# Linear attention in a 16-part network: one masked copy of the queries for each tile, scores over 32 rows, values in two strips, and another draw of the order

## What is computed

```python
def titans_forward(hidden_states, Wq, Wk, Wv, conv_q, conv_k, conv_v, W_init, ln_gamma, ln_beta, Wg, Wo, num_heads=16, chunk_size=16):
    q = l2norm(jax.nn.silu(short_conv(hidden_states @ Wq.T, conv_q)).reshape(b, l, h, dk))
    ...
    def step(W, chunk):
        q_c, k_c, v_c = chunk
        inter = jnp.einsum('bqhk,bhkv->bqhv', q_c, W)
        qk = jnp.einsum('bqhd,bkhd->bhqk', q_c, k_c) * mask
        intra = jnp.einsum('bhqk,bkhv->bqhv', qk, v_c)
        W_new = W + jnp.einsum('bchk,bchv->bhkv', k_c, v_c)
        return (W_new, inter + intra)
    ...
    o = (o - mu) * jax.lax.rsqrt(var + EPS_LN) * ln_gamma + ln_beta
    gate = hidden_states @ Wg.T
    return o * gate @ Wo.T
```

## Time and profile before

| | before |
|---|---|
| median of 3 runs | 3529.78 us (3524.93 to 3536.67) |
| the profiled execution | 3542.59 us, span 3541.3 us, clock 0.933 |
| PE busy | 3005.1 us, 85% |
| DVE busy | 2370.4 us, 67% |
| ACT busy | 2252.9 us, 64% |
| POOL busy | 1280.5 us, 36% |
| granted TensorE clock, mean | 0.933 |
| instructions | 56793 |

### The profile page before, as it was taken

How to read it: one execution, slowest core, us unless ns; L and a number is a source line. 1 busy time by engine, 2 the same in 40 slices (tenths; PEclk the granted TensorE clock), 3 DMA queues, 4 the chain that set the end, 5 groups by cost and what they waited for, 6 DMA issues and landing times. The chain is left out here.

```text
span 3541.3 us, 56793 instructions
## 1 busy us (share of the span) xinstructions
PE 3005.1 (85%) x20199; PEld 1965.9 (56%) x20199; DVE 2370.4 (67%) x6076; ACT 2252.9 (64%) x4884; POOL 1280.5 (36%) x1196
## 2 busy tenths in 40 slices
PE   3577899898989999999998777787988879899997
PEld 2356666665645555555564454664746648555444
DVE  4888755566678777676777888776454443566655
ACT  3556564536756776667777775874847746567764
POOL 2555533523445643243564654443020120211221
PEclk9789999999999999999999998998999979899998
DMA  6444422222100012110101213554342234222320
GB/s 245 129 124 146 118 70 82 72 60 83 55 11 1 1 33 53 40 46 15 52 1 34 73 58 96 161 150 114 101 108 88 79 102 142 77 67 51 74 56 7
DMA packets 209444, 272.22 MB, mean 77 GB/s; under 512 B 39560, under 2 KB 147272, under 8 KB 207176
## 3 DMA queue, kind: packets, MB, share of 16 engines
q1 hardware_dynamic: 200968, 251.79, 24.5%
q0 software_dynamic: 8192, 16.79, 1.6%
HBM read 217.02 MB, written 54.00 MB: 77 GB/s over the span
## 5 line engine op out<-in xcount | busy, mean ns | idle before, releaser
L382 ACT ACTIVATE scratch<-psum 128x512 f32<-128x512 f32 (+7 forms) x1804 | 837.3, 495 | 695.4 <-PE psum L328 483.5
L328 PE MATMUL psum<-scratch 128*128 128x128 f32 (+14 forms) x8016 | 936.8, 321 | 110.8 <-ACT scratch L382 34.6
L474 POOL TENSOR_TENSOR scratch<-scratch 128x512 f32<-128x512 f32 (+3 forms) x536 | 615.1, 1162 | 753.1 <-PE psum L353 280.4
L328 PEld LDWEIGHTS psum<-scratch 128*32 128x32 f32 (+7 forms) x8016 | 592.4, 147 | 435.0 <-issue 192.4
L382 ACT ACTIVATE scratch<-scratch 128x512 f32<-128x512 f32 (+8 forms) x856 | 395.2, 468 | 230.9 <-DVE scratch L404 143.3
L374 ACT ACT_TABLE_LOAD x390 | 500.4, 1283 | 17.8 <-DVE scratch L404 8.0
L404 DVE TENSOR_TENSOR scratch<-psum,scratch 128x512 f32<-128x512 f32 (+3 forms) x712 | 381.2, 547 | 149.6 <-ACT scratch L382 109.3
L348 PE MATMUL psum<-w_constants,scratch 128*128 128x128 f32 (+1 forms) x1944 | 329.1, 290 | 48.9 <-ACT scratch L382 17.3
L418 DVE TENSOR_TENSOR_SCAN psum<-psum,scratch 128x512 f32<-128x512 f32 x256 | 309.2, 1222 | 70.4 <-ACT psum L382 59.9
L427 DVE TENSOR_REDUCE scratch<-psum 128x2 f32<-128x512 f32 (+2 forms) x336 | 225.0, 677 | 193.8 <-PE psum L328 158.2
L382 ACT ACTIVATE psum<-scratch 128x255 f32<-128x255 f32 (+1 forms) x528 | 221.2, 457 | 171.2 <-DVE scratch L404 161.1
(11 more groups left out here) (108 smaller groups left out, 4214.0 us busy)
## 6 DMA issues: line engine op xcount, KB each, us to landing
scratch<-b_and_c_out SPq DMA_DIRECT2D x256, 256.0 KB
scratch<-L_experts_rows_dram SPq DMA_DIRECT2D x56, 544.0 KB
scratch<-L_experts_rows_dram SPq DMA_DIRECT2D x56, 514.0 KB
slots_out<-scratch SPq DMA_DIRECT2D x112, 128.0 KB
q_stack<-scratch SPq DMA_DIRECT2D x72, 192.0 KB, 2.5
scratch<-q_out SPq DMA_DIRECT2D x96, 96.0 KB
scratch<-slots_in SPq DMA_DIRECT2D x16, 512.0 KB
q_out<-scratch SPq DMA_DIRECT2D x40, 192.0 KB, 3.0
```

The source lines that it names most:

```text
L328: return self.engine.matmul(out, lhsT, rhs, start=start, stop=stop, **kw)
L382: return self.engine.activation(out, src, function, **kw)
L474: return self.engine.tensor_tensor(out, a, b, op)
```

## The change

One constant now says which of four places within its group a channel has, for all groups at once, so a single masked copy `qm` holds for a tile what four copies did. The scores of group g take only the group's 32 rows of `k` and of this copy; 64 copies on POOL become 16. `st` gets three buffers, the third in `padded`, which is not used by then. The values of two groups form one step, `pe_intra`, in which the matmuls alternate between two 32-column strips of the array; PE's order in a tile is scores 0, 1, 2, values of groups 0 and 1, scores 3, values of groups 2 and 3. The seed of the draw is 3, and the planner takes the load of the masks to be complete 2000 ns later.

```diff
--- before.py
+++ after.py
@@ -70,7 +70,7 @@
 
 
     c["head_of_col_group"] = np.tile((ch[None] % 32 // HD8 == np.arange(4)[:, None]).astype(float).reshape(1, -1), (P, 1))
-    c["channels_of_head"] = (np.arange(HEADS8)[None] == ch[:, None] // HD8).astype(float)
+    c["place_in_group"] = (np.arange(4)[None] == ch[:, None] % 32 // HD8).astype(float)
     q, k = np.arange(P)[:, None], np.arange(P)[None]
     c["keys_up_to_query"] = (q <= k).astype(float)
 
@@ -514,7 +514,7 @@
 
 
 
-    LEFT, NEAR, DRAW = 0.4, 3.0, 20
+    LEFT, NEAR, DRAW = 0.4, 3.0, 3
 
     def __init__(self, nc, ctx):
         self.nc, self.ctx, self.draws = nc, ctx, np.random.RandomState(self.DRAW)
@@ -957,7 +957,10 @@
         self.v_tok, self.k_tok = self.take(TILES, P), self.take(PER_STREAM, P)
         self.state = self.take(P)
         self.o = self.v
-        self.qm, self.st, self.vm = [self.take(4, P), self.take(4, P)], self.take(4, P), self.take(4, P)
+        self.qm, self.vm = [self.take(4, P), self.take(4, P)], self.take(4, P)
+        mark = self.used
+        self.st = [self.take(4, P), self.take(4, P), v2(self.padded.rearrange("p a b -> p (a b)")[:, 0:4 * P], P)]
+        self.used = mark
         self.out_norm = Norm(self, "o", self["o", TILES - 1], self.o, self.o, self.c["center8"], self.c["mean8"],
                              eps[:, 0:1], self.w["ln_gamma"], self.w["ln_beta"])
 
@@ -990,23 +993,30 @@
                 e.wait_ge(*(yield self["o", t - 1]))
             e.matmul(self.b[:, 0:P], self.state if chunk else w["state0"], self.q[:, here], skip_group_check=True)
             for g in range(4):
-                rows = slice(32 * g, 32 * g + 32)
-                e.wait_ge(*(yield self["one_head", t, g]))
+                if g == 0:
+                    e.wait_ge(*(yield self["one_head", t]))
                 if g:
                     e.wait_ge(*(yield self["masked", t, g - 1]))
                 elif t:
                     e.wait_ge(*(yield self["masked", t - 1, 3]))
-                e.matmul(self.a, self.k[:, here], self.qm[g % 2].rearrange("p a b -> p (a b)")).then_inc(*self.post("scores", t, g))
-                e.wait_ge(*(yield self["masked", t, g]))
-                e.wait_ge(*(yield self["spread_v", t]))
-                for j in range(4):
-                    last = e.matmul(self.b[rows, 0:P], self.vm[:, j, rows], self.st[:, j, :], start=False, skip_group_check=True)
-                last.then_inc(*self.post("intra", t, g))
+                e.matmul(self.a, self.k[32 * g:32 * g + 32, here], self.qm[t % 2][32 * g:32 * g + 32].rearrange("p a b -> p (a b)")).then_inc(*self.post("scores", t, g))
+                if g >= 2:
+                    yield from self.pe_intra(e, t, g - 2)
         yield from self.out_norm.pe(e)
         e.wait_ge(*(yield self["normed", "o"]))
         e.matmul(self.a, w["Wg"], self.xn).then_inc(*self.post("gate"))
         e.wait_ge(*(yield self["gated"], None, (self.b, self["norm", "logvar", "o"])))
         e.matmul(self.b, w["Wo"], self.o).then_inc(*self.post("out"))
+
+    def pe_intra(self, e, t, pair):
+
+        e.wait_ge(*(yield self["masked", t, 2 * pair + 1]))
+        e.wait_ge(*(yield self["spread_v", t]))
+        for j in range(4):
+            for g in (2 * pair, 2 * pair + 1):
+                rows = slice(32 * g, 32 * g + 32)
+                last = e.matmul(self.b[rows, 0:P], self.vm[:, j, rows], self.st[(4 * t + g) % 3][:, j, :], start=False, skip_group_check=True)
+        last.then_inc(*self.post("intra", t, pair))
 
     def act(self, e):
         T = TOKENS
@@ -1023,7 +1033,7 @@
         e.wait_ge(*(yield self["tokens"]))
         e.activation(self.k_tok, v2(self.b[:, 0:PER_STREAM * P], P), ACT.Copy).then_inc(*self.post("token", "k_tok"))
         for t in range(TILES):
-            e.wait_ge(*(yield self["intra", t, 3]))
+            e.wait_ge(*(yield self["intra", t, 1]))
             e.activation(self.o[:, t * P:(t + 1) * P], self.b[:, 0:P], ACT.Copy).then_inc(*self.post("o", t))
         yield from self.out_norm.act(e)
 
@@ -1053,11 +1063,10 @@
                 e.tensor_tensor(self.state, self.state, w["state0"], ALU.add).then_inc(*self.post("state", t))
             for g in range(4):
                 e.wait_ge(*(yield self["scores", t, g]))
-                if g:
-                    e.wait_ge(*(yield self["intra", t, g - 1]))
-                elif t:
-                    e.wait_ge(*(yield self["intra", t - 1, 3]))
-                e.tensor_tensor(self.st, v2(self.a, P), over(self.c["keys_up_to_query"].unsqueeze(1), [P, 4, P]), ALU.mult).then_inc(*self.post("masked", t, g))
+                n = 4 * t + g - 3
+                if n >= 0:
+                    e.wait_ge(*(yield self["intra", n // 4, n % 4 // 2]))
+                e.tensor_tensor(self.st[(4 * t + g) % 3], v2(self.a, P), over(self.c["keys_up_to_query"].unsqueeze(1), [P, 4, P]), ALU.mult).then_inc(*self.post("masked", t, g))
         yield from self.out_norm.dve(e)
         e.wait_ge(*(yield self["gate"]))
         e.tensor_tensor(self.o, self.o, self.a, ALU.mult).then_inc(*self.post("gated"))
@@ -1066,18 +1075,16 @@
 
     def pool(self, e):
         e.wait_ge(*(yield self["normed", "k"]))
-        for n in range(4 * TILES):
-            t, g = divmod(n, 4)
-            if n >= 2:
-                e.wait_ge(*(yield self[("scores", *divmod(n - 2, 4))]))
-            q = self.q[:, t * P:(t + 1) * P]
-            e.tensor_tensor(self.qm[g % 2], over(q.unsqueeze(1), [P, 4, P]),
-                            over(self.c["channels_of_head"][:, 4 * g:4 * g + 4].unsqueeze(2), [P, 4, P]), ALU.mult).then_inc(*self.post("one_head", t, g))
-            if g == 0:
-                e.wait_ge(*(yield self["token", "v_tok"]))
-                if t:
-                    e.wait_ge(*(yield self["intra", t - 1, 3]))
-                e.tensor_tensor(self.vm, over(self.v_tok[:, t:t + 1, :], [P, 4, P]), v2(self.c["head_of_col_group"], P), ALU.mult).then_inc(*self.post("spread_v", t))
+        for t in range(TILES):
+            here = slice(t * P, (t + 1) * P)
+            if t >= 2:
+                e.wait_ge(*(yield self["scores", t - 2, 3]))
+            e.tensor_tensor(self.qm[t % 2], over(self.q[:, here].unsqueeze(1), [P, 4, P]),
+                            over(self.c["place_in_group"].unsqueeze(2), [P, 4, P]), ALU.mult).then_inc(*self.post("one_head", t))
+            e.wait_ge(*(yield self["token", "v_tok"]))
+            if t:
+                e.wait_ge(*(yield self["intra", t - 1, 1]))
+            e.tensor_tensor(self.vm, over(self.v_tok[:, t:t + 1, :], [P, 4, P]), v2(self.c["head_of_col_group"], P), ALU.mult).then_inc(*self.post("spread_v", t))
 
 
 def row_exp_dve(b, e, tag, ready, logits, out, m, n):
@@ -3197,7 +3204,7 @@
             e.dma_start(weights["constants"].buf, packed_dram["constants"]).then_inc(*core.post((0, "load", "constants"), 16, FIRST_LATENCY))
             first, *rest = [g for g in groups[1:] if g not in LATER]
             e.dma_start(weights[first].buf, packed_dram[first]).then_inc(*core.post((0, "load", first), 16, FIRST_LATENCY))
-            e.dma_start(staged, packed_dram["masks"]).then_inc(*core.post((0, "load", "masks"), 16, FIRST_LATENCY))
+            e.dma_start(staged, packed_dram["masks"]).then_inc(*core.post((0, "load", "masks"), 16, FIRST_LATENCY + 2000))
             e.dma_start(x[:, COLS:], x_dram[:, COLS:]).then_inc(*core.post((0, "load", "x_rest"), 16, FIRST_LATENCY))
             for g in rest:
                 e.dma_start(weights[g].buf, packed_dram[g]).then_inc(*core.post((0, "load", g), 16, LOAD_LATENCY))
```

## The result

The changed kernel takes 3547.1 us against 3532.4, the medians of 20 executions each: ratio 1.0041, interval 1.0029 to 1.0052. It is slower by 0.4%, 15 us, where a gain of 17 was forecast. Its profiled execution took 3550.4 us, span 3549.0, clock 0.925.

What follows compares the result with a forecast made beforehand. PE's time was taken as the first limit of the Linear stage, one stream's chain as the second. Of 20 us saved on PE 15 reach the end, with 2 from the start: -17, median 3529.8 to 3513; range 3482 to 3550.

Steps and rivals of the forecast that it cites:

- (6): Whole kernel: the new draw breaks ties differently, moving the end 18 us either way, centre 0.
- the sum: Whole kernel: 15 of 20 us saved on PE reach the end, plus 2 from the start: -17 us.
- (1): Linear's values on PE: 32 lots in two strips at 1.22 us replace 64 at 1.18; gain 36.5 us.
- The rival without overlap: Linear's values: strips do not run side by side, PE loses 13 us, time 3538; chance 0.03.
- (2): Linear's scores on PE: 32 rows lengthen each slot by 0.28 us, 64 times: 18 us of loss.
- the rival: Linear stage: emptier array lowers PE's clock; at 0.85 the kernel takes 3547 us; chance 0.09.
- point of balance: Linear stage: clock of 0.90, where PE's slowdown equals the 20 us saved.
- (3): One stream's Linear chain: a tile falls from 11.1 to 8.75 us, saving 10.6 us over four tiles.
- a sign of being wrong: After Linear: the prediction is wrong if Linear shortens and the lead is gone later.
- (4): POOL in Linear: 64 masked query copies become 16, 50 us less work, costed at nothing; bounds 0 to -2 us.
- (5): Kernel start on ACT: square precedes the masks' conversion, logarithm at 16.6 instead of 18.61, 2.0 us earlier.
- slower by the order: Outside the Linear stage: the draw costs its 18 us and more and eats the gain, 3550; chance 0.12.

Runs made afterwards that it cites:

- five orders: Five settings of seed or masks' due time, each run without and with the Linear edits in the full kernel; mean difference 0.05%, standard error 0.4%.
- Linear alone: Network replaced by eight Linear parts per stream, seed 3: 1536.3 us without edits, 1557.2 with all three, 1843.0 with only 32-row scores.
- strips alone: Linear-only kernel before plus values in pairs of strips and three masked copies of scores, scores on 128 rows, 64 query copies: 1308.6 us.

## Why the prediction was wrong

Two steps failed. Term (6) put the new draw at a centre of 0, and without any edit of Linear the new seed and due time made the kernel before 1.3% slower, about 45 us. And the sum let 15 us of PE's gain reach the end, where over five orders nothing did (2 us slower in the mean, standard error 14): the lower clock that comes with 32-row scores takes part of the gain, and the lead that remains is lost in later parts. Term by term:

- (1) Values in strips: right. Two strips run side by side, 36.6 us busy for 512 records; the slot is 1.19 by the forecast's own count (1.22 forecast), so the term was 37 for such a lot (36.5 forecast). The rival without overlap is out. Linear alone gained 28.5 a pass by it.
- (2) Scores over 32 rows: incomplete. The slot is right within its bounds, 15 to 25 us of loss for 18. But I priced the shape only by what neighbours lose around it and took the clock as given. Linear alone shows 38 us a pass without and 31 with the strips (1557 less 1309, over 8), not 18, and most of it is clock. In the full kernel the stage's clock (380 to 800) is 0.94 to 1.00 in the eight profiles with scores on 128 rows, mean 0.965, and 0.90 to 0.94 in the six with 32 rows, mean 0.922; at like seed and due time it is lower with 32 rows in all five orders. By my own figure for the rival, 403 us of work at full clock, 403/0.922 - 403/0.965 is 20 us: the 20 us of PE that the sum gained. In the pair compared here it fell only from 0.943 to 0.931, which is 6 us. That rival had a chance of 0.09 and should have been a term. It named the right thing, yet its point of balance, 0.90, was not reached in the changed kernel, and it left out that the clock without the edit would have been above 0.94 in most orders.
- (3) The chain: the Linear parts are 22 us shorter in the mean, within the 10 to 25 forecast, and the wait in front of the values fell from 11.0 to 0.2 us. This length is real in all five orders and did not help: that three quarters of a local gain reach the end was wrong. Nothing of the 18 us lead at 956 us was left at 2238, which the prediction had named as a sign of being wrong.
- (4) POOL: 48 us less, at no visible price; with 128 rows and the single copy Linear alone was as fast as with strips alone.
- (5) Start: right in mechanism, better in size. ACT's timeline of the kernel after:

```profile
10.23 1.28 ACT L382 ACT_TABLE_LOAD   x1 [10.23 <-PE psum L328]
11.52 0.60 ACT L382 ACTIVATE scratch<-psum 128x512 f32<-128x512 f32 x1
12.01 2.52 ACT L382 ACTIVATE bf_masks<-scratch 128x2786 bf16<-128x2786 f32 x1
...
15.84 0.69 ACT L382 ACTIVATE scratch<-psum,w_constants 128x512 f32<-128x512 f32 x1
```

  The square goes ahead of the conversion and the logarithm starts at 15.84 instead of 18.61, 2.8 us earlier, 0.7 of which come from an earlier first product (10.11 instead of 10.78). The same edit in the kernel before made the whole 1.4% slower: a due time is a draw like a seed.
- (6) The draw: the term that decided the sign. I gave it 18 us either way from the spread of one part and a centre of 0. Its standard deviation is 35 us, and seed 20 lay 0.7% below the mean of its column, so the centre was some 24 us on the slow side. The rival "slower by the order" with 0.12 is what happened: without the edits the new seed and due time give 1.0128* (not repeated at the 3532 to 3540 level; there the seed alone gives 1.0125 and 1.0169 and the due time alone 1.0141). With the edits it came to 1.0041: in this one order they are worth -0.8%, in two others as much the other way, so it is luck that the time is not further up. The measured time of 3547 lies inside the range of 3482 to 3550.

How the 15 us divide between edits and order has no exact answer, since each order gives the edits another worth, from -0.8% to +1.1%. Not shown is why the lead of Linear is lost before the second scan, as it is in the mean of the five orders, and which feature of an order makes it slow.

## What to carry to other kernels

- Where a planner with random ties makes the order, compare an edit over several draws on both sides. One draw on each side measures the draws, here 1.0% against a local gain of half a per cent. Trying seeds on the unedited kernel was worth more (0.8%, seen in one batch) than the edit.
- A matmul cut to fewer rows gained no time here (a slot of 1.25 us where 128 rows took 0.87). Before cutting, look whether the granted clock of the stage has anything to lose; with scores in a quarter of the rows it went from 0.99 to 0.83 with PE 92% busy in both.
- A shorter part is a gain only where the row that follows it shows the lead kept. Compare the mean over all streams at each part's end, since a single stream's lead of 58 us said nothing.

## What the runs showed of the hardware beyond that

- Two column strips of 32 give 16 float32 records of 128 columns in 1.07 us; one strip gave 8 in the same time.
- The same kernel, before, took 3532 to 3540 us in three batches and 3421 to 3423 in three others, 3.3% less. Its granted clock differed too, 0.93 to 0.94 in the former and 0.95 to 0.96 in the latter. Matmuls last about as long in both (the 1800 with constants and 128 columns 290 ns in the mean in before's profile, 288 in that of the kernel with seed 3 and the later due time). Over all profiles of the full network, each kernel another order, most of the difference lies behind the second scan's adds: that stretch takes 1303 to 1357 us in the former batches and 1212 to 1301 in the latter, all ahead of it 2219 to 2254 and 2169 to 2241. The cause was not found.
